# SyncE fetches one packed tile in six row by row, beside ScalarE's, in a graph layer on one Trainium2 core

## The chip, the cores and the metric

The kernel runs on one core of one Trainium2 chip. The metric is the time of one execution in microseconds (us) on the device, as a median of runs. The engines are called PE (TensorE), DVE (VectorE), ACT (ScalarE), POOL (GpSimd) and SP (SyncE). A queue name such as ACTq or SPq stands for what that engine's instruction stream issues to the DMA engines.

## What is computed

A graph layer over 12500 nodes of 128 features and 212500 edges, sorted by destination. Each edge carries the source node's row, multiplied by one of eight matrices that its type selects; the results are summed at the destination; a GRU cell updates the node; a residual and a layer norm follow. Cut to the core:

```python
all_msgs = jnp.einsum('nh,thd->ntd', h, message_W) + message_b
msg = all_msgs[src, edge_type]
messages = jax.ops.segment_sum(msg, dst, num_segments=num_nodes)
gi = messages @ gru_w_ih.T + gru_b_ih          # split in i_r, i_z, i_n
gh = h @ gru_w_hh.T + gru_b_hh                 # split in h_r, h_z, h_n
r = sigmoid(i_r + h_r); z = sigmoid(i_z + h_z); n = tanh(i_n + r * h_n)
out = layernorm(x + (1 - z) * n + z * h)       # h is x
```

## The kernel before

**Tiles and rounds.** Edges are taken in tiles of 128. The first 187 tiles (rounds 0 to 10, 17 tiles each) are "early". While they run, DVE packs the other edges on the chip (edges from a node to itself are taken out), and from round 11 on each round takes 16 packed tiles. There are 98 rounds, 0 to 97 (LAST), all written out without a loop. A round has three groups, of 6, 5 and 5 tiles in the packed part (GROUPS). Round r also finishes node tiles of some rounds before: the gates of node tile r-2, and the update and norm of r-3.

**A tile's way.** The 128 source rows of a tile, 512 bytes each, are brought from x in DRAM into SBUF, node on partition. PE multiplies them by a one-hot matrix of (destination, type) into the PSUM bank of the group (`sum_tiles`, L1651). ACT copies the bank out (L726), PE applies the eight matrices (`apply_weights`, L1678), DVE adds the window to the running sums in SBUF (L1166).

**Who brings the rows.** Nearly all tiles come by an indirect DMA that POOL issues, one for a tile (L660, called from `gather_packed`). Even and odd packed rounds have row sets of their own: `rows` for rounds 11, 13, ..., `rows_other` for 12, 14, .... So POOL, before it gathers group c of round r, waits only until PE has done group c of round r-2. One tile in every six rounds, the last of group 2 in rounds 17, 23, ..., 95 (FETCH_ROUNDS, 14 rounds), is not gathered by POOL. ACT fetches it during the six rounds up to and with its own: `fetch_rows` reads row numbers from SBUF into registers and issues one DMA a row (L896), 16 rows at one place of the round and 8 at another (8 only in the last of the six). These rows go to slot 16 of `rows`, which is otherwise free. PE waits for them on the semaphore `fetched`. The row numbers themselves are brought by SP, one line of 128 numbers a tile (`load_fetch_index`, L561).

**SP's round.** From round 12 on SP runs `round_(r)`: load x_next for node tile r (L544, waits until PE has turned the one before, L1687), store the finished node tile r-3 (L557, waits for DVE's out_tile, L1271), load x_tile for node tile r-2 (L548, under the same condition, read by DVE at L1251 in the next round). After a fetch round it adds one L561.

**Order on the other engines.** In a packed round PE runs: turn x (L1687), counts (L1616), group 0, the weights of the round before (L1678, L1680), group 1, group 2, then the gates of node tile r-2 (L1697, L1709, L1712, L1717). ACT runs the update of r-3, `fetch_rows(r, 0)`, copies of counts and sums, and `fetch_rows(r, 1)` after group 1.

Of the kernel before, what the change touches and what calls it, by code (L numbers as in the profile page):

```python
# [5 lines left out]
P = 128  # L6
F32 = mybir.dt.float32
BF16 = mybir.dt.bfloat16
I32 = mybir.dt.int32
# [7 lines left out]
def gnn_kernel(nc, x, src, dst, etype, w_msg, b_msg, w_ih, w_hh, b_ih, b_hh, out):  # L17
    ds = bass.ds
    NODES, HID = x.shape
# [8 lines left out]
    LAG = 2  # L28


    EARLY = 11
# [21 lines left out]
    LAST = ROUNDS - 1  # L53
# [5 lines left out]
    SPARE_SLOT = ROUND  # L59
# [6 lines left out]
    FETCH_EVERY = 6  # L66
    FETCH_AHEAD, FETCH_BEHIND = 16, 8
    FETCH_ROUNDS = tuple(range(EARLY + FETCH_EVERY, LAST, FETCH_EVERY))
    FETCH_SLOT = (ROUND - 1) % ROW_TILES
    FETCH_STEP = FETCH_EVERY * ROUND // ROW_TILES  # L70
    FETCH_TILE = GROUPS[2] - 1
# [35 lines left out]
    with ctx:  # L107
        def sb(name, shape, dt=F32):
            return ctx.enter_context(nc.sbuf_tensor(name, shape, dt))
# [4 lines left out]
        def sem(name):  # L114
            return ctx.enter_context(nc.semaphore(name))
# [69 lines left out]
        w_hh_rows = sb("w_hh_rows", [P, 3, HID])  # L185
# [6 lines left out]
        bias_part = [sb(f"bias_part{n}", [1, 512], BF16) for n in range(PARTS)]  # L192
# [5 lines left out]
        rows = sb("rows", [P, EARLY_ROUND, HID])  # L198
# [23 lines left out]
        fetch_src = w_ih_rows[:, 0, :].bitcast(I32)  # L222
        fetch_index = bias_part[0][0:1, :].bitcast(I32).rearrange("o (s e) -> o s e", e=P)

        def sets(name, cols, dt=F32):
            return [sb(f"{name}{s}", [P, cols], dt) for s in range(2)]

# [93 lines left out]
        fetch_src_ready = sem("fetch_src_ready")  # L321
        fetch_index_in = [sem(f"fetch_index_in{s}") for s in range(2)]
        fetched = [sem(f"fetched{s}") for s in range(2)]
        tiles_first_ready = sem("tiles_first_ready")
        tiles_first_in = sem("tiles_first_in")
        packed_code_ready = sem("packed_code_ready")
# [10 lines left out]
        tiles_done = [sem(f"tiles_done{c}") for c in range(3)]  # L337
# [78 lines left out]
        offset_lots = [(row, a, min(row.shape[1], SPARE_TILE + 1 - a))  # L416
                       for row, a in ((gate_bias, 0), (bias_rest, 512), (bi_row, 1024))]
        assert offset_lots[-1][1] + offset_lots[-1][2] == SPARE_TILE + 1

        def fetches(r):  # L420
            return isinstance(r, int) and r in FETCH_ROUNDS

# [66 lines left out]
        def _(sp):  # L489
# [65 lines left out]
            def store_out(j, n=P, s=0):  # L555
                sp.wait_ge(out_ready, j + 1)
                sp.dma_start(out[ds(j * P, n), :], out_tile[s][0:n, :]).then_inc(out_stored, 16)  # L557

            def load_fetch_index(m):
                row = (m + 1) * FETCH_STEP + 1  # L560
                sp.dma_start(fetch_index[0:1, m % 2, :], fetch_src[row:row + 1, :]).then_inc(fetch_index_in[m % 2], 16)  # L561

            def round_(r):
                load_x(r)
                store_out(r - LAG - 1)
                load_x_tile(r - LAG)

            flag = load_flag(sp)
            with sp.If(flag):
                last = NODE_TILES - 1  # L570
                load_x(0)
                load_x_tile(0)
                sp.dma_start(x_tile[1][0:NODE_LAST, :], x[last * P:NODES, :]).then_inc(last_x_tile_in, 16)
                load_bias()
                load_x(1)
                sp.wait_ge(packing, AT["next"])
                with nc.allow_non_contiguous_dma(reason="the kind of the edge that follows the early ones"):
                    sp.dma_start(kinds_T[P - 1:P, EARLY_TILES - 1, 1:2], moves_f[0:1, 0:1]).then_inc(carried, 16)
                load_x(2)
                for r in range(LAG + 1, EARLY - 1):  # L580
                    round_(r)
                sp.wait_ge(tiles_first_ready, 1)
                sp.wait_ge(fields_turned, CHUNKS)
                sp.dma_start(first_packed[0:1, 0:PACKED_TILES].rearrange("o (r k) -> o r k", k=ROW_TILES),
                             row_tiles_first[0:ROWS, :]).then_inc(tiles_first_in, 16)
                sp.wait_ge(fields_turned, FIELDS * CHUNKS)
                sp.dma_start(loops_words.rearrange("o (p c) -> o p c", c=WINDOW),
                             zeros_f[0:ACC_ROWS // 2 // WINDOW, 0:WINDOW]).then_inc(loops_zero, 16)
                for r in range(EARLY - 1, EARLY + 1):
                    round_(r)  # L590
                sp.wait_ge(fetch_src_ready, 1)
                sp.wait_ge(bias_in, PARTS * 16)
                for m in range(2):
                    load_fetch_index(m)
                for r in range(EARLY + 1, LAST):
                    round_(r)
                    m = (r - EARLY) // FETCH_EVERY + 1
                    if fetches(r - 1) and m < len(FETCH_ROUNDS):
                        sp.wait_ge(tiles_done[2], r)
                        load_fetch_index(m)  # L600
                load_x(last, NODE_LAST)
                store_out(last - LAG - 1)
                load_x_tile(last - LAG)
                sp.dma_start(last_x_tile, x[(last - 1) * P:last * P, :]).then_inc(last_x_tile_in, 16)
                store_out(last - LAG)
                store_out(last - 1)
                store_out(last, NODE_LAST, 1)
                sp.wait_ge(out_stored, 16 * NODE_TILES)
# [36 lines left out]
        def _(pool):  # L645
# [30 lines left out]
            def gather_packed(r):  # L676
                for c, n, start in groups(r):
                    pool.wait_ge(tiles_done[c], r if r == EARLY else r - 1)
                    for k in range(start, start + n - (c == 2 and fetches(r))):
                        a = column(r, k)  # L680
                        gather((rows_other if other(r) else rows)[:, k, :], src_T[:, a:a + 1],
                               gathered_last[k] if r == LAST else (gathered_other if other(r) else gathered)[c])
# [10 lines left out]
            with pool.If(flag):  # L693
# [5 lines left out]
                for r in range(EARLY, ROUNDS):  # L699
                    gather_packed(r)  # L700
                pool.wait_ge(tiles_done[2], FETCH_ROUNDS[-1] + 1)
                gather(rows[:, SPARE_SLOT, :], src_T[:, SPARE_COL:SPARE_COL + 1], gathered_last[SPARE_SLOT])
# [851 lines left out]
        def _(pe):  # L1554
# [71 lines left out]
            def landed(r, c):  # L1626
                if r < EARLY:
                    return max(1, r - 1) * EARLY_GROUPS[c]
                alike = range(EARLY + other(r), r + 1, 2)
                left_out = sum(fetches(q) for q in alike) if c == 2 else 0  # L1630
                return (0 if other(r) else (EARLY - 2) * EARLY_GROUPS[c]) + len(alike) * GROUPS[c] - left_out

            def sum_tiles(r, c, offs):
                _, n, start = groups(r)[c]
                if r > 0:
                    pe.wait_ge(sums_copied[c], r)
                pe.wait_ge(onehot_ready[c], r + 1)
                ahead = isinstance(r, int) and r in (1, 2)
                place = (rows, rows_second, rows_third)[r] if ahead else rows_other if other(r) else rows
                if ahead:  # L1640
                    pe.wait_ge(gathered_ahead[c], r * n * 16)
                elif r < LAST:
                    pe.wait_ge((gathered_other if other(r) else gathered)[c], landed(r, c) * 16)
                for k in range(n):
                    if r == LAST:
                        pe.wait_ge(gathered_last[start + k], 16)
                    slot = start + k
                    if fetches(r) and c == 2 and k == FETCH_TILE:
                        m, slot = (r - EARLY) // FETCH_EVERY - 1, SPARE_SLOT
                        pe.wait_ge(fetched[m % 2], (m // 2 + 1) * P * 16)  # L1650
                    last = nc.tensor.matmul(agg[c][:, ds(offs[c][k] * TYPES, CODES)],  # L1651
                                            place[:, slot, :],
                                            onehot[c][:, k, :], start=False, stop=True, skip_group_check=True)
                if isinstance(r, int) and r == LAST and c == 2:
                    pe.wait_ge(last_tile_ready, 3)
                    pe.wait_ge(gathered_last[SPARE_SLOT], 16)
                    last = nc.tensor.matmul(agg[2][:, ds(offs[3][0] * TYPES, CODES)], rows[:, SPARE_SLOT, :],
                                            onehot[1][:, GROUPS[1], :], start=False, stop=True, skip_group_check=True)
                last.then_inc(tiles_done[c], 1)
# [163 lines left out]
            with pe.Else():  # L1823
# [11 lines left out]
                with pe.Fori(0, EDGE_TILES) as i:  # L1835
# [5 lines left out]
                    for h, bank in enumerate((agg[2], cnt)):  # L1841
# [4 lines left out]
                                                start=False, stop=True)  # L1846
# [42 lines left out]
```

## Time and profile before

| | us |
|---|---|
| median of 3 runs | 1994.47 |
| lowest and highest | 1990.95, 1996.48 |
| profiled execution, own time | 1993.74 |
| its span | 1991.6 |

The times are of the whole execution. The profile's times count from the start of the span, which is 2.14 us shorter than the profiled execution's own time. Busy times are sums over an engine's instructions; "issue" is idle time for which the profile shows no releaser. A line of a timeline is: start, duration, engine, source line, operation, tiles written and read, how many were merged, and in brackets the idle time before it with what ended it.

### The profile page before, as it was taken

How to read it: one execution, taken by the hardware profiler on the slowest of the kernel's cores; microseconds unless marked ns; L12 is line 12 of the kernel's file. 1: busy time of each engine (PE TensorE's matmuls, PEld its weight loads, DVE VectorE, ACT ScalarE, POOL GpSimd, SP SyncE). 2: the span in 40 equal slices, each digit the busy share in tenths (PEclk: the TensorE clock that was granted, in tenths of full speed). 3: DMA queues.
4: the chain of work that ended last, by engine and by line, in shares of the span. 5: the costliest groups of instructions: out<-in, count | busy, mean ns of one | idle time of the engine just before them, and what ended most of it. 6: DMA issues, size and time to landing. Idle time of an engine off the chain costs nothing.

```text
span 1991.6 us, 34610 instructions
## 1 busy us (share of the span) xinstructions
PE 1372.3 (69%) x6657; PEld 1045.8 (53%) x6657; DVE 1245.0 (63%) x4650; ACT 595.0 (30%) x1489; POOL 1488.7 (75%) x1578
## 2 busy tenths in 40 slices
PE   1766676767676767676767777767676766766676
PEld 1755555555555555455545555545455555555554
DVE  7887465656565656565656566656565656565566
ACT  2323423232323232323232323232222323232222
POOL 7777777777777777777777777777777777777774
PEclk9877878888888888787878888888888888888889
DMA  5222222222222222222222222222222222222221
GB/s 128 58 62 64 56 64 65 66 62 64 63 66 61 65 63 65 62 65 62 66 61 66 63 65 63 64 63 65 63 64 63 64 63 63 63 65 63 64 63 45
DMA packets 100626, 128.44 MB, mean 64 GB/s; under 512 B 33280, under 2 KB 74959, under 8 KB 100478
## 3 DMA queue, kind: packets, MB, share of 16 engines
q0 software_dynamic: 50112, 102.73, 19.8%
q1 hardware_dynamic: 46584, 23.07, 4.2%
q10 hardware_dynamic: 3782, 0.93, 0.2%
q8 instruction: 61, 1.00, 0.2%
q14 instruction: 87, 0.71, 0.1%
HBM read 120.16 MB, written 6.40 MB: 64 GB/s over the span
## 4 chain that ended last, share of the span: by engine, by line
POOL 65%; issue 22%; DVE 8%; PE 3%; ACT 1%; DMA 1%; DVEq 0%; SPq 0%; ACTq 0%; POOLq 0%
POOL rows_other L660 33%; POOL rows L660 32%; DVE work L1317 1%; DVE codes L1314 1%; PE agg L1651 1%; DVE onehot L1150 1%; PE msg L1678 1%; DMA work<-in_src_dram 0%; DVE root_a L1224 0%; DVE messages_T L1166 0%; ACT sums_room L726 0%; ACT agg L726 0%; DVEq L1157 0%; PE gates L1717 0%; PE turn L1733 0%
## 5 line engine op out<-in xcount | busy, mean ns | idle before, releaser
L660 POOL DMA_INDIRECT rows<-in_x_dram,src_T x843 | 801.2, 950 | 260.9 <-issue 256.1
L660 POOL DMA_INDIRECT rows_other<-in_x_dram,src_T x688 | 651.8, 947 | 209.8 <-issue 209.8
L1651 PE MATMUL agg<-onehot,rows 128*128 128x128 f32 x1714 | 288.0, 330 | 256.9 <-DMA rows<-in_x_dram,src_T 255.9
L1678 PE MATMUL msg<-sums_room,w_type 128*128 128x320 f32 (+1 forms) x1552 | 443.1, 442 | 13.8 <-issue 10.3
L1651 PE MATMUL agg<-onehot,rows_other 128*128 128x128 f32 x1376 | 232.7, 330 | 259.6 <-DMA rows_other<-in_x_dram,src_T 258.3
L1651 PEld LDWEIGHTS agg<-onehot,rows 128*128 128x128 f32 x1714 | 259.6, 236 | 277.6 <-issue 276.6
L1678 PEld LDWEIGHTS msg<-sums_room,w_type 128*128 128x128 f32 x1552 | 306.2, 205 | 122.3 <-issue 27.0
L1199 DVE SCALAR_TENSOR_TENSOR sums_room<-turn,x_turned 128x128 f32<-128x128 f32 x696 | 145.6, 281 | 350.7 <-PE turn L1697 350.7
L1651 PEld LDWEIGHTS agg<-onehot,rows_other 128*128 128x128 f32 x1376 | 208.2, 235 | 278.5 <-issue 278.5
L726 ACT ACTIVATE sums_room<-agg 128x512 f32<-128x512 f32 x293 | 173.3, 591 | 375.7 <-PE agg L1651 327.6
L1150 DVE TENSOR_TENSOR onehot<-code_T,codes 128x640 f32<-128x640 f32 (+1 forms) x294 | 244.3, 859 | 18.9 <-PE agg L1651 18.8
L726 ACT ACTIVATE x_turned<-cnt 128x128 f32<-128x128 f32 x97 | 26.9, 277 | 670.9 <-PE msg L1680 573.9
L726 ACT ACTIVATE agg<-zeros_f 128x512 f32<-128x512 f32 x294 | 176.6, 601 | 9.4
L1138 DVE TENSOR_TENSOR node_mask<-rel_T,codes 128x320 bf16<-128x320 f32 (+3 forms) x294 | 139.1, 473 | 0.0
L1712 PE MATMUL gates<-w_hh_T,x_T 128*128 128x384 f32 x194 | 126.8, 751 | 0.0
L1166 DVE TENSOR_TENSOR messages_T<-messages_T,msg 128x64 f32 x291 | 63.9, 219 | 79.3 <-PE msg L1680 46.8
L1717 PE MATMUL gates<-w_ih_T,messages 128*128 128x384 f32 x194 | 107.5, 646 | 1.9 <-DVE messages L1207 1.9
L1177 DVE TENSOR_TENSOR loop_counts<-counts,loop_row 1x192 f32<-1x192 f32 x87 | 30.4, 350 | 97.1 <-ACT loop_row L726 87.6
L1616 PEld LDWEIGHTS cnt<-node_mask,type_mask 128*128 128x128 bf16 (+1 forms) x783 | 64.4, 105 | 47.6 <-issue 24.7
L1616 PE MATMUL cnt<-node_mask,type_mask 128*128 128x128 bf16 (+1 forms) x783 | 86.9, 228 | 0.0
L1717 PEld LDWEIGHTS gates<-w_ih_T,messages 128*128 128x128 f32 x194 | 54.5, 282 | 51.4 <-issue 42.8
L1181 DVE TENSOR_TENSOR work<-work,loop_counts 1x64 f32 x261 | 56.4, 216 | 37.3 <-DVE loop_counts L1177 0.2
(219 smaller groups left out, 1357.0 us busy)
## 6 DMA issues: line engine op xcount, KB each, us to landing
rows<-in_x_dram ACTq DMA_DIRECT2D x1792, 0.5 KB
rows<-in_x_dram,src_T POOLq DMA_INDIRECT x843, 2.5
rows_other<-in_x_dram,src_T POOLq DMA_INDIRECT x688
x_next<-in_x_dram SPq DMA_DIRECT2D x97, 64.0 KB
out_dram<-out_tile SPq DMA_DIRECT2D x97, 64.0 KB
x_tile<-in_x_dram SPq DMA_DIRECT2D x96, 64.0 KB
work<-in_dst_dram SPq DMA_DIRECT2D x1, 609.4 KB
work<-in_src_dram SPq DMA_DIRECT2D x1, 609.4 KB
```

The lines of the kernel that those rows point to most:

```text
L660: nc.gpsimd.indirect_dma_start(out=to, out_offset=None, in_=x[:, :], in_offset=bass.IndirectOffsetOnAxis(ap=index, axis=0),).then_inc(done ...
L726: return nc.scalar.activation(to, value, ACT.Copy)
L1138: nc.vector.tensor_tensor(node_mask[c][:, 0:n, 0:wide], rel_T[:, cols].unsqueeze(2).broadcast_to([P, n, wide]), codes[:, 0:wide].unsqueeze ...
L1150: nc.vector.tensor_tensor(onehot[c][:, 0:n, :], code_T[:, ds(column(r, start), n)].unsqueeze(2).broadcast_to([P, n, CODES]), codes[:, 0:CO ...
L1166: ins = nc.vector.tensor_tensor(messages_T[:, ds(node, WINDOW)], messages_T[:, ds(node, WINDOW)], bank[:, c * WINDOW:(c + 1) * WINDOW], AL ...
L1181: ins = nc.vector.tensor_tensor(loops_T[:, ds(node, WINDOW)], loops_T[:, ds(node, WINDOW)], (loop_counts if since(r, EARLY) else counts)[0 ...
L1199: done = nc.vector.scalar_tensor_tensor(out=to[:, t, :], in0=turn[:, 0:P], scalar=t - NO_LOOP, in1=values, op0=ALU.is_equal, op1=ALU.mult)
L1616: last = nc.tensor.matmul(cnt[0:m * HALF, c * P:c * P + m * WINDOW], type_mask[c][:, k:k + m, :].rearrange("p k t -> p (k t)"), node_mask[ ...
L1651: last = nc.tensor.matmul(agg[c][:, ds(offs[c][k] * TYPES, CODES)], place[:, slot, :], onehot[c][:, k, :], start=False, stop=True, skip_gr ...
L1678: nc.tensor.matmul(msg[:, 0:cols], w_type[:, t, :], sums[:, t, 0:cols], start=t == 0, stop=False, skip_group_check=True)
L1712: nc.tensor.matmul(bank[:, HID:4 * HID], x_lhs, w_hh_T[:, :], start=False, stop=False)
L1717: nc.tensor.matmul(gates_of(j)[:, 0:GATE], value, w_ih_T[:, :], start=False, stop=True).then_inc(gates_ready, 1)
```

## The change

SP takes over the last tile of group 2 in 13 further rounds: 20, 26, ..., 92 (SYNC_ROUNDS), which lie three rounds apart from ACT's. In these rounds POOL gathers 15 tiles rather than 16. SP fetches the 128 rows over six rounds, 8 right after its x_next load and 16 after its x_tile load (8 in all in the last of the six), each with a DMA of its own whose row number is read from SBUF into a register. The rows go to a room of their own, 512 bytes a partition that held a part of w_hh, which nobody reads after the start. PE waits for them on `sync_fetched` ahead of that tile's product. The 128 row numbers of each tile come by one more small load on SP; from the second tile on it stands behind a wait of SP for `tiles_done[2]` at r. All that ACT fetches stays as it was.

```diff
+    SYNC_ROUNDS = tuple(range(EARLY + FETCH_EVERY + FETCH_EVERY // 2, LAST, FETCH_EVERY))
...
+        sync_index = bias_part[1][0:1, :].bitcast(I32).rearrange("o (s e) -> o s e", e=P)
+        sync_room = w_hh_rows[:, 0, :]
...
+            def load_sync_index(m):
+                row = (m + 1) * FETCH_STEP + FETCH_STEP // 2 + 1
+                sp.dma_start(sync_index[0:1, m % 2, :], fetch_src[row:row + 1, :]).then_inc(sync_index_in[m % 2], 16)
+
+            def sync_rows(r, behind):
+
+                m, step = divmod(r - EARLY - FETCH_EVERY // 2 - 1, FETCH_EVERY)
+                if m < 0 or m >= len(SYNC_ROUNDS) or behind and sync_fetches(r):
+                    return
+                a = step * (FETCH_AHEAD + FETCH_BEHIND) + behind * FETCH_BEHIND
+                n = FETCH_AHEAD if behind else FETCH_BEHIND
+                if step == 0 and not behind:
+                    sp.wait_ge(sync_index_in[m % 2], (m // 2 + 1) * 16)
+                    if m > 0:
+                        sp.wait_ge(tiles_done[2], r)
+                        if m + 1 < len(SYNC_ROUNDS):
+                            load_sync_index(m + 1)
+                _, numbers = nc.values_load_multi_w_load_instructions(
+                    sync_index[0:1, m % 2, a:a + n], engines=[sp.engine], min_val=0, max_val=NODES - 1,
+                    skip_runtime_bounds_check_because="row numbers, as the gathers take them")
+                for p, number in enumerate(numbers, a):
+                    sp.dma_start(sync_room[p:p + 1, :], x[ds(number, 1), :]).then_inc(sync_fetched[m % 2], 16)
...
                 for m in range(2):
                     load_fetch_index(m)
+                    load_sync_index(m)
                 for r in range(EARLY + 1, LAST):
-                    round_(r)
+                    load_x(r)
+                    sync_rows(r, 0)
+                    store_out(r - LAG - 1)
+                    load_x_tile(r - LAG)
+                    sync_rows(r, 1)
...
-                    for k in range(start, start + n - (c == 2 and fetches(r))):
+                    for k in range(start, start + n - (c == 2 and (fetches(r) or sync_fetches(r)))):
...
-                left_out = sum(fetches(q) for q in alike) if c == 2 else 0
+                left_out = sum(fetches(q) or sync_fetches(q) for q in alike) if c == 2 else 0
...
+                    elif sync_fetches(r) and c == 2 and k == FETCH_TILE:
+                        m, tile_rows = (r - EARLY) // FETCH_EVERY - 1, sync_room
+                        pe.wait_ge(sync_fetched[m % 2], (m // 2 + 1) * P * 16)
```

## Rows read from the trace of the kernel before

**Rows 1.** The page's first part: span, and busy time of each engine.

```profile
span 1991.6 us, 34610 instructions
PE 1372.3 (69%) x6657; PEld 1045.8 (53%) x6657; DVE 1245.0 (63%) x4650; ACT 595.0 (30%) x1489; POOL 1488.7 (75%) x1578
```

**Rows 2.** The page's chain that ended last, shares of the span by engine.

```profile
POOL 65%; issue 22%; DVE 8%; PE 3%; ACT 1%; DMA 1%; DVEq 0%; SPq 0%; ACTq 0%; POOLq 0%
```

**Rows 3.** Groups of instructions on POOL, 262 us to 1972 us: count, busy, mean ns, idle.

```profile
L660 POOL DMA_INDIRECT rows_other<-in_x_dram,src_T x688 | 651.8, 947 | 209.8 <-issue 209.8
L660 POOL DMA_INDIRECT rows<-in_x_dram,src_T x678 | 642.1, 947 | 206.8 <-issue 206.8
```

**Rows 4.** POOL's timeline: last wait for PE, an ACT-fetch round, a plain round, the end.

```profile
243.64 0.94 POOL L660 DMA_INDIRECT rows<-in_x_dram,src_T  x1 [3.54 <-PE agg L1651]
...
602.79 0.94 POOL L660 DMA_INDIRECT rows<-in_x_dram,src_T  x1 [0.30 <-issue]
...
620.28 1.11 POOL L660 DMA_INDIRECT rows<-in_x_dram,src_T  x1 [0.31 <-issue]
621.69 0.94 POOL L660 DMA_INDIRECT rows_other<-in_x_dram,src_T  x1 [0.30 <-issue]
...
641.69 0.94 POOL L660 DMA_INDIRECT rows<-in_x_dram,src_T  x1 [0.30 <-issue]
...
1949.18 0.94 POOL L660 DMA_INDIRECT rows_other<-in_x_dram,src_T  x1 [0.30 <-issue]
...
1970.41 0.94 POOL L660 DMA_INDIRECT rows<-in_x_dram,src_T  x1 [0.30 <-issue]
```

**Rows 5.** PE's timeline over that ACT-fetch round and the start of the next.

```profile
608.95 0.27 PE L1687 MATMUL cnt<-ident,x_next 128*128 128x128 f32 x1
609.05 0.95 PE L1616 MATMUL cnt<-node_mask,type_mask 128*128 128x128 bf16 x9
611.65 1.58 PE L1651 MATMUL agg<-onehot,rows 128*128 128x128 f32 x12 [1.65 <-DMA rows<-in_x_dram,src_T]
613.07 4.47 PE L1678 MATMUL msg<-sums_room,w_type 128*128 128x320 f32 x16
617.38 0.49 PE L1680 MATMUL msg<-counts,b_type 128*128 128x192 f32 x2
618.03 1.35 PE L1651 MATMUL agg<-onehot,rows 128*128 128x128 f32 x10 [0.16 <-DMA rows<-in_x_dram,src_T]
623.02 2.48 PE L1651 MATMUL agg<-onehot,rows 128*128 128x128 f32 x10 [3.64 <-DMA rows<-in_x_dram,src_T]
...
628.57 0.27 PE L1687 MATMUL cnt<-ident,x_next 128*128 128x128 f32 x1
```

**Rows 6.** Groups on PE, 262 us to 1950 us: the tile products and their waits.

```profile
L1651 PE MATMUL agg<-onehot,rows_other 128*128 128x128 f32 x1366 | 231.2, 330 | 256.1 <-DMA rows_other<-in_x_dram,src_T 254.7 <-issue 0.2
L1651 PE MATMUL agg<-onehot,rows 128*128 128x128 f32 x1376 | 230.0, 328 | 238.7 <-DMA rows<-in_x_dram,src_T 237.8
```

**Rows 7.** ACT's timeline around its row fetches.

```profile
610.71 0.28 ACT L842 ACTIVATE gates<-t_pre 128x128 f32<-128x128 f32 x1 [0.93 <-DVE t_pre L1240]
611.60 3.03 ACTq L896 DMA_DIRECT2D rows<-in_x_dram  x8
...
629.89 0.28 ACT L842 ACTIVATE gates<-t_pre 128x128 f32<-128x128 f32 x1 [0.48 <-DVE t_pre L1240]
631.24 6.08 ACTq L896 DMA_DIRECT2D rows<-in_x_dram  x16
```

**Rows 8.** SP's timeline, two rounds with the next start, then its tightest later round.

```profile
609.25 0.33 SPq L544 DMA_DIRECT2D x_next<-in_x_dram  x1
615.41 0.34 SPq L557 DMA_DIRECT2D out_dram<-out_tile  x1
615.80 0.43 SPq L548 DMA_DIRECT2D x_tile<-in_x_dram  x1
628.87 0.33 SPq L544 DMA_DIRECT2D x_next<-in_x_dram  x1
634.59 0.34 SPq L557 DMA_DIRECT2D out_dram<-out_tile  x1
634.98 0.43 SPq L548 DMA_DIRECT2D x_tile<-in_x_dram  x1
635.46 0.51 SPq L561 DMA_DIRECT2D bias_part<-w_ih_rows  x1
...
728.49 0.33 SPq L544 DMA_DIRECT2D x_next<-in_x_dram  x1
734.43 0.34 SPq L557 DMA_DIRECT2D out_dram<-out_tile  x1
734.82 0.45 SPq L548 DMA_DIRECT2D x_tile<-in_x_dram  x1
745.19 0.33 SPq L544 DMA_DIRECT2D x_next<-in_x_dram  x1
```

**Rows 9.** SP's own waits, 262 us to 1950 us: total, times, longest.

```profile
SPq L544 <- PE cnt L1687: 1109.5, 86, 19.9
SPq L557 <- DVE out_tile L1271: 463.6, 83, 7.0
```

**Rows 10.** DVE's timeline: the reader of x_tile.

```profile
630.30 0.29 DVE L1251 TENSOR_TENSOR t_d<-x_tile,gates 128x128 f32<-128x128 f32 x1 [0.44 <-ACT gates L842]
```

**Rows 11.** Busy time in stretches; the last three columns are PEclk, DMA share, GB/s.

```profile
265.00:1950.00 1685.00, 1184.33 (x5620) 888.06 (x5620) 1025.29 (x3928) 494.66 (x1278) 1274.83 (x1346) 0.84 0.24 64
```

**Rows 12.** Groups on POOL, 1950 us to 1972 us, where ACT fetches no rows.

```profile
L660 POOL DMA_INDIRECT rows<-in_x_dram,src_T x17 | 16.1, 945 | 5.2 <-issue 5.2
```

**Rows 13.** The page's DMA queues: packets, MB, share of 16 engines' span.

```profile
q10 hardware_dynamic: 3782, 0.93, 0.2%
```

**Rows 14.** PE's timeline at the end: last wait for a gather, and the last rounds' products.

```profile
1951.79 1.46 PE L1651 MATMUL agg<-onehot,rows_other 128*128 128x128 f32 x10 [3.56 <-DMA rows_other<-in_x_dram,src_T]
...
1974.57 1.28 PE L1651 MATMUL agg<-onehot,rows 128*128 128x128 f32 x10
```

More of the change, by code:

```diff
@@ L323, in gnn_kernel @@
         fetched = [sem(f"fetched{s}") for s in range(2)]
+        sync_index_in = [sem(f"sync_index_in{s}") for s in range(2)]
+        sync_fetched = [sem(f"sync_fetched{s}") for s in range(2)]
         tiles_first_ready = sem("tiles_first_ready")
@@ L418, in gnn_kernel, with sync_fetches @@
         assert offset_lots[-1][1] + offset_lots[-1][2] == SPARE_TILE + 1
+        def sync_fetches(r):
+            return isinstance(r, int) and r in SYNC_ROUNDS
         def fetches(r):
@@ L1646, in sum_tiles @@
                         pe.wait_ge(gathered_last[start + k], 16)
-                    slot = start + k
+                    tile_rows = place[:, start + k, :]
                     if fetches(r) and c == 2 and k == FETCH_TILE:
-                        m, slot = (r - EARLY) // FETCH_EVERY - 1, SPARE_SLOT
+                        m, tile_rows = (r - EARLY) // FETCH_EVERY - 1, rows[:, SPARE_SLOT, :]
                         pe.wait_ge(fetched[m % 2], (m // 2 + 1) * P * 16)
+                    elif sync_fetches(r) and c == 2 and k == FETCH_TILE:
+                        m, tile_rows = (r - EARLY) // FETCH_EVERY - 1, sync_room
+                        pe.wait_ge(sync_fetched[m % 2], (m // 2 + 1) * P * 16)
                     last = nc.tensor.matmul(agg[c][:, ds(offs[c][k] * TYPES, CODES)],
-                                            place[:, slot, :],
+                                            tile_rows,
                                             onehot[c][:, k, :], start=False, stop=True, skip_group_check=True)
```

## The prediction, made before the changed kernel ran

> **What bounds the kernel now.** I read the busy times first [rows 1]: POOL is the busiest engine, but 75% alone would leave a quarter of the span open. The chain that ended last closes that gap [rows 2]: 65% of the span is POOL and 22% is "issue", 87% together. The groups on POOL say what this issue time is [rows 3]: 1366 gathers of 947 ns, and before them 209.8 + 206.8 = 416.6 us of idle time, all of it "issue", so 305 ns ahead of each gather and no wait for any engine. The timeline gives the same [rows 4]: POOL waits for PE the last time at 243.64 us and then issues one gather after another. One gather costs POOL 947 + 305 = 1252 ns. A plain round of 16 gathers, from 621.69 to 641.69 us [rows 4], gives 20.00 / 16 = 1.250 us. Whatever takes one gather out of this stretch, and leaves nothing else late, takes 1.25 us out of the time.
>
> PE follows behind. Its products of tiles wait 254.7 + 237.8 = 492.5 us for landings in 262 to 1950 us [rows 6], over 85 rounds 5.8 us each. In a round these waits lie at 1.65, 0.16 and 3.64 us ahead of the three groups [rows 5]. The small one is no sign of a bound: PE may be late for group 1 as long as it has caught up at group 2, where 3.64 us are left. And POOL doesn't feel PE's lag. It starts to refill `rows` at 641.69, where PE had read group 0 of that set from 611.65 for 1.58 us: 28.5 us of room.
>
> **What is removed.** 13 gathers, in rounds 20, 26, ..., 92. All of them lie behind 243.64 us and ahead of 1949.18, so on the chain. 13 x 1.252 = **16.3 us**. That a round with 15 gathers is really shorter is shown by ACT's fetch round: POOL starts `rows` at 602.79 and the next set at 621.69, so 18.90 us, with one long gather of 1.11 us among the 15; the plain round behind it lasts 641.69 - 621.69 = 20.00 us [rows 4]. The difference is 1.10 us, and 1.26 us without the 0.16 us of the long gather. The rest of that round on PE bears it too: group 2 with the fetched tile takes 2.48 us with nothing between its ten products [rows 5], so a wait for fetched rows ahead of the fifth tile costs nothing where the rows are there.
>
> **The end.** It moves as a whole. The last wait for a gather is at 1951.79, for the gather of 1949.18; from there on PE is never again held by POOL [rows 14], though the last gather is issued until 1971.35 (1970.41 + 0.94). By the 1.67 us that passed between the end of the gather of 1949.18 (1950.12) and its landing at 1951.79, that last one lands at about 1973.0, and PE takes up the products that need it at 1974.57. Its margin of 1.5 us stays, since POOL and PE both arrive 16.3 us earlier; nothing of the gain is lost there. The end's 1991.6 - 1951.8 = 39.8 us stay as they are.
>
> **What is added on SP.** 24 rows a round in five rounds of six and 8 in the sixth, over 78 rounds (15 to 92). SP issues no such DMA before, so the price is ACT's: 6.08 us for 16 and 3.03 us for 8, 0.38 us a row, and between the last work and the first row 631.24 - 630.17 = 1.07 us for 16 register loads and 611.60 - 610.99 = 0.61 us for 8 [rows 7]. Bounds for a row on SP: its own shortest DMA is 0.33 us and its own longest 0.51 us [rows 8]. I take 0.38, since it is the same kind of instruction; the range keeps both ends. SP's round is then:
> x_next 0.33, registers 0.61, 8 rows 3.03: SP is ready for the store 3.97 us after the start. It now starts the store 615.41 - 609.25 = 6.16 us after, held by DVE's out_tile; over all rounds this wait is 463.6 / 83 = 5.6 us [rows 9]. So the 3.64 us disappear in it, with 2 us to spare. At 0.51 us a row it would be 4.7 of 5.6 us: still hidden.
> Store 0.34, x_tile 0.43 to 0.45, registers 1.07, 16 rows 6.08: the last two, 7.15 us, come ahead of the next x_next. The room there is 628.87 - 616.23 = 12.6 us in the shown round, 1109.5 / 86 = 12.9 us on average [rows 9], and 745.19 - 735.27 = 9.9 us in the tightest round behind 300 us [rows 8]. At 0.51 us it would be 9.2 us, just inside.
> A whole SP round is 0.33 + 0.61 + 3.03 + 0.34 + 0.43 + 1.07 + 6.08 = 11.9 us of the 19.6 us between two x_next loads. What is queued behind the rows keeps its time: the store and x_tile wait for DVE anyway, x_tile issued at 615.80 is read at 630.30 [rows 10], and x_next of 609.25 at 628.57 [rows 5].
> **SP's new wait** for `tiles_done[2]` at r is met when it is reached: SP has just passed the wait for PE's turn in round r (L1687), and PE does that turn after group 2 of round r-1. Behind it are the index load (0.51 us, 13 in all, two of them at the start of round 12 beside ACT's two) and the 8 rows; 3.97 + 0.51 = 4.5 us is still under 5.6. Cost nothing.
>
> **What is added on PE and the DMA engines.** Thirteen waits on PE, in rounds with 3.6 us or more of room. The last 8 rows of a tile are issued from 0.9 us to 4.0 us after PE's turn; PE reaches the fifth tile of group 2 some 15 us after it (623.02 + 4/5 x 2.48 - 608.95 = 16.1 us). ACT's last 8 go out 0.6 us later than that (611.60 to 614.63) and are in time. The traffic is small: ACT's 1792 rows are q10's 3782 packets, at 0.2% of 16 engines' span [rows 13], so 0.002 x 16 x 1991.6 = 64 us or 36 ns a row. 1664 rows more are 59 us of DMA time, spread over 1500 us. The 16 DMA engines are busy 24% of the time [rows 11].
> **A gather beside them** could take longer. The nearest rows: 947 ns while ACT fetches [rows 3] and 945 ns where it doesn't [rows 12]. Were SP's rows to add the same 2 ns to all 1366 gathers, that is 2.7 us; below, a gain isn't to be had, for the 945 ns are as low as any. I take nothing, since single gathers spread more (0.94 to 1.11), and keep 2.7 us in the range.
>
> Sum: 1993.74 - 16.3 = 1977.4 us for an execution like the profiled one. The median of the runs shown is 0.73 us above the profiled execution: 1994.47 - 16.3 = **1978.2 us**, 0.8% faster.
>
> **A rule that speaks against it.** What would be bound if the DMA engines were full, not POOL? The trace says 24% busy and 1.25 us a gather on POOL [rows 3, 11]. The Trainium skill, page "DMA: Bandwidth & Descriptors", section "Issuing engines are not separate DMA queues", says that DMAs started on several engines run on the same 16 DMA engines, and that spreading them saves only the starting engine's time, "which is usually small relative to the DMA itself". By that rule the change would bring nothing and the time would stay 1994.5 us. Here the rule's first half may well hold, but not its "small": the starting time is what fills POOL.
>
> **Rivals.**
> 1. *SP becomes the bound, slower than before.* A row costs SP much more than ACT. SP's round is 2.8 us plus 24 rows, against a round of 19.6 us, so it decides from (19.6 - 2.8) / 24 = 0.70 us a row. At 0.80 us SP's round is 22.0 us against the 20.0 of a plain one, in 65 rounds of 24 rows: 65 x 2.0 = 130 us more, 2124 us. Against it: SP's own DMAs of 128 rows each take 0.33 to 0.51 us. Chance 0.03.
> 2. *Gathers stretch and eat the gain: no change.* The gain is gone if 1366 gathers take 16.3 / 1366 = 12 ns more each, by more descriptors on the shared engines: 1994.5 us. For it: POOL's work is itself a DMA's start, and the rule above; against it: the 2 ns between stretches with and without ACT's rows. A half-way form, 6 ns, would give 1986 us. Chance 0.05 for a loss beyond 10 us.
> 3. *PE waits for SP's rows.* Rows that go out in single DMAs behind 64 KB transfers on the same queue could land 12 us late. Then PE stands in 13 rounds; but since POOL has 28 us of room, only PE's own lag counts, which 3.6 us a round take back. Only a wait of over 28 us reaches POOL. Time 1978 us as in the forecast, so it changes nothing but a wait. Its bad form, rows missing for more than that: chance 0.01, slower.
>
> **Chances.** Forecast, faster: 0.91. Rival 2, within 0.3%: 0.05. Rivals 1 and 3, slower: 0.03 + 0.01 = 0.04. A difference of 0.3%, 6 us, is about what a measurement of this kernel can tell from no change. The forecast's own range is 1978.2 less 3 us and plus 2.7 + 3 us, where 3 us is the spread of the runs before around their median (1990.95 to 1996.48): 1975 to 1984. I widen it a little below, for a disturbance that the median of three holds: 1974 to 1984.
>
> **What would show it.** Right: 13 gathers fewer on POOL, each still 945 to 948 ns with 305 ns idle; "issue" the only releaser; rounds of 18.8 us at every third place and of 20.0 between them; SP with 1664 row DMAs at 0.33 to 0.51 us; SP's wait at L544's place fallen from 12.9 to about 5.8 us on average, at L557's from 5.6 to about 2; the wait on PE a little smaller (about 5.6 us a round) and always for gathers. Wrong: x_next late on PE, an idle time on POOL that PE ends, a gather mean above 950 ns, or a PE wait that ends with `sync_room`.

## The result, and the profile after the change

The changed kernel took 1975.4 us (median of 4 runs, 1974.54 to 1976.46), the kernel before 1994.0 us. The ratio is 0.991 (95% interval 0.9897 to 0.9922): 0.9% faster, where 1978.2 us and 0.8% had been forecast. Two later comparisons, told below, gave 0.9909 (0.9892 to 0.9926) and again 0.9909 (0.9893 to 0.9926).

The span and the chain of the changed kernel, to be laid beside [rows 1, 2]:

```profile
span 1973.7 us, 39661 instructions
PE 1356.7 (69%) x6561; PEld 1050.8 (53%) x6657; DVE 1248.0 (63%) x4650; ACT 594.6 (30%) x1489; POOL 1474.7 (75%) x1565
...
POOL 65%; issue 22%; DVE 8%; PE 3%; ACT 1%; DMA 1%; DVEq 0%; SPq 0%; ACTq 0%; POOLq 0%
```

POOL has 13 instructions less (1565 for 1578), and the chain is made of the same parts: what bounded the kernel bounds it still. POOL's groups from 262 us to 1956 us answer to [rows 3]:

```profile
L697 POOL DMA_INDIRECT rows<-in_x_dram,src_T x676 | 639.5, 946 | 206.2 <-issue 206.2
L697 POOL DMA_INDIRECT rows_other<-in_x_dram,src_T x675 | 638.1, 945 | 205.9 <-issue 205.9
```

There is still no releaser but "issue", so POOL never waited in this stretch. POOL's timeline, the first gather of round 12 and the last of round 96, answers to the end in [rows 4]:

```profile
263.22 0.94 POOL L697 DMA_INDIRECT rows_other<-in_x_dram,src_T  x1 [0.30 <-issue]
...
1929.11 0.94 POOL L697 DMA_INDIRECT rows_other<-in_x_dram,src_T  x1 [0.30 <-issue]
```

In the kernel before the same two stood at 265.04 and 1949.18 us:

```profile
265.04 0.95 POOL L660 DMA_INDIRECT rows_other<-in_x_dram,src_T  x1 [0.30 <-issue]
```

That a round with 15 gathers is the shorter one shows in the first gathers of rounds 31, 32 and 33, of which 32 is one of SP's:

```profile
637.09 0.94 POOL L697 DMA_INDIRECT rows<-in_x_dram,src_T  x1 [0.30 <-issue]
...
657.08 0.94 POOL L697 DMA_INDIRECT rows_other<-in_x_dram,src_T  x1 [0.30 <-issue]
...
675.96 0.94 POOL L697 DMA_INDIRECT rows<-in_x_dram,src_T  x1 [0.30 <-issue]
```

Round 31 takes 19.99 us and round 32 takes 18.88.

So the 17.9 us between the spans (1991.6 - 1973.7) come apart in three: the stretch between these gathers fell from 1684.14 to 1665.89 us, by 18.25; what lies ahead of it is 1.82 us shorter (265.04 to 263.22); what lies behind, from the last of them to the end of the span, is 2.17 us longer (42.42 to 44.59).

SP's own part, two rounds of its timeline in the changed kernel, beside [rows 7, 8]:

```profile
604.80 0.36 SPq L553 DMA_DIRECT2D x_next<-in_x_dram  x1
606.10 3.48 SPq L589 DMA_DIRECT2D w_hh_rows<-in_x_dram  x8
610.85 0.38 SPq L566 DMA_DIRECT2D out_dram<-out_tile  x1
611.28 0.42 SPq L557 DMA_DIRECT2D x_tile<-in_x_dram  x1
613.09 6.48 SPq L589 DMA_DIRECT2D w_hh_rows<-in_x_dram  x16
624.47 0.36 SPq L553 DMA_DIRECT2D x_next<-in_x_dram  x1
```

16 rows take 6.48 us, 0.405 a row here; the 8 take 3.48 us, 0.435 a row, but most batches of 8 take about 3.15. The register loads lie in the gaps: 606.10 - 605.16 = 0.94 us for 8, and 613.09 - 611.70 = 1.39 us for 16. After the last row, at 619.57, SP stands idle for 4.9 us until the next x_next. The waits of SP from 262 us to 1935 us answer to [rows 9]:

```profile
SPq L553 <- PE cnt L1727: 567.0, 86, 20.4
SPq L566 <- DVE out_tile L1308: 140.4, 84, 6.8
```

Ahead of x_next 567.0 / 86 = 6.6 us are left of 12.9, ahead of the store 140.4 / 84 = 1.7 us of 5.6. The new work went into SP's waits, as it was meant to.

### The profile page after: what moved, and what is told of

It reads as the page before. It is cut to its first block, busy times and chain, and to the rows that moved or that the text cites. A ratio compares the mean times of both kernels' runs of the same rounds, so it can differ in the third digit from the quotient of the medians.

```text
span 1973.7 us, 39661 instructions
## 1 busy us (share of the span) xinstructions
PE 1356.7 (69%) x6561; PEld 1050.8 (53%) x6657; DVE 1248.0 (63%) x4650; ACT 594.6 (30%) x1489; POOL 1474.7 (75%) x1565
## 4 chain that ended last, share of the span: by engine, by line
POOL 65%; issue 22%; DVE 8%; PE 3%; ACT 1%; DMA 1%; DVEq 0%; SPq 0%; ACTq 0%; POOLq 0%
POOL rows L697 32%; POOL rows_other L697 32%; DVE work L1354 1%; DVE codes L1351 1%; PE agg L1691 1%; DVE onehot L1187 1%; PE msg L1718 1%; DMA work<-in_src_dram 0%; PE msg L1836 0%; DVE root_a L1261 0%; DVE messages_T L1203 0%; ACT sums_room L763 0%; PE turn L1773 0%; ACT agg L763 0%; DVEq L1194 0%
## 5 line engine op out<-in xcount | busy, mean ns | idle before, releaser
L697 POOL DMA_INDIRECT rows_other<-in_x_dram,src_T x675 | 638.1, 945 | 205.9 <-issue 205.9
L1691 PE MATMUL agg<-onehot,rows_other 128*128 128x128 f32 x1350 | 224.6, 326 | 230.5 <-DMA rows_other<-in_x_dram,src_T 229.0
L1691 PEld LDWEIGHTS agg<-onehot,rows_other 128*128 128x128 f32 x1350 | 200.9, 231 | 248.2 <-issue 248.1
L1187 DVE TENSOR_TENSOR onehot<-code_T,codes 128x640 f32<-128x640 f32 (+1 forms) x294 | 245.2, 863 | 18.2 <-PE agg L1691 18.2
L1757 PE MATMUL gates<-w_ih_T,messages 128*128 128x384 f32 x194 | 115.1, 688 | 2.2 <-DVE messages L1244 2.2
```

What stands on the lines that cost most here:

```text
L697: nc.gpsimd.indirect_dma_start(out=to, out_offset=None, in_=x[:, :], in_offset=bass.IndirectOffsetOnAxis(ap=index, axis=0),).then_inc(done ...
L1187: nc.vector.tensor_tensor(onehot[c][:, 0:n, :], code_T[:, ds(column(r, start), n)].unsqueeze(2).broadcast_to([P, n, CODES]), codes[:, 0:CO ...
L1757: nc.tensor.matmul(gates_of(j)[:, 0:GATE], value, w_ih_T[:, :], start=False, stop=True).then_inc(gates_ready, 1)
```

## The experiments

Two theories were to be told apart. Mine: the time is POOL's count of gathers times 1.25 us, and SP's rows cost nothing. The rival: SP's rows do something to the gathers or to the loads, and the sum only happens to come out. Beside them stood the question from which point SP's own time binds. The lines of these kernels are numbered a little differently; the names are the same.

**First chip.** The first four kernels ran together on a chip on which the kernel before took 2451.2 us. It has no trace there; in the kernels that have one, POOL isn't what bounds them. They are told first, since they showed something that no later run did.

*The cost alone.* POOL gathers all tiles as before and PE reads POOL's copy, while SP fetches its rows and PE waits for them:

```diff
-                    for k in range(start, start + n - (c == 2 and (fetches(r) or sync_fetches(r)))):
+                    for k in range(start, start + n - (c == 2 and fetches(r))):
...
-                        m, tile_rows = (r - EARLY) // FETCH_EVERY - 1, sync_room
+                        m = (r - EARLY) // FETCH_EVERY - 1
                         pe.wait_ge(sync_fetched[m % 2], (m // 2 + 1) * P * 16)
```

> The cost alone: SP fetches its 1664 rows and PE waits for them, but POOL gathers all tiles as before and PE reads POOL's copy. My theory (only POOL's gathers set the time, SP's rows are hidden): as before, 1994 us, within 2 us; gathers of 945 to 948 ns. Rival (SP's rows change how long a gather takes): with the 1.5 ns less a gather that the changed kernel's trace shows, 1992 us; with 12 ns more, 2010 us.

It took 2609.3 us, ratio 1.0632 (1.0602 to 1.0662) to the kernel before on that chip. Neither theory had this.

*The gain alone.* POOL leaves out the 13 gathers, and `load_sync_index` and `sync_rows` are not called:

```diff
-                        m, tile_rows = (r - EARLY) // FETCH_EVERY - 1, sync_room
-                        pe.wait_ge(sync_fetched[m % 2], (m // 2 + 1) * P * 16)
+                        tile_rows = sync_room
```

> The gain alone: POOL leaves out the 13 gathers and SP fetches nothing; PE multiplies what lies in the room, without a wait, so the rows of these 13 tiles are left out of the result. My theory: 1994 - 13 x 1.25 = 1977.7 us, and at most 2 us from the changed kernel's 1975.4, so 1975 to 1978. Rival (SP's rows cost something that is hidden in the sum, by shared DMA engines or late loads): clearly below the changed kernel, 1970 us or less.

It took 2430.4 us, ratio 0.9919 (0.9897 to 0.994). The ratio is much like the forecast's, but POOL isn't the bound there, and in what way 13 gathers less shorten this kernel is not shown. The chain of this kernel on that chip, by engine and by line, shows ACT's row fetches (L930) in POOL's place:

```profile
issue 33%; ACTq 33%; ACT 12%; DVE 9%; PE 8%; another core or an unknown queue 2%; DVEq 1%; DMA 0%; SPq 0%
ACTq L930 28%; ACT sums_room L760 5%; ACTq L926 4%; PE msg L1714 3%; PE agg L1687 2%; ACT counts L760 2%; ACT loop_row L760 1%; ACT gates L876 1%; PE gates L1753 1%; DVEq L1191 1%; PE gates L1748 1%; ACT agg L760 1%; DVE onehot L1184 1%; DVE work L1351 1%
```

A row is three instructions on ACT: two of registers, then the DMA. The durations of the first and the last of them (ns, lowest, median and highest), first in the changed kernel where the kernel before takes 1994 us, then in this one on the first chip:

```profile
L933 ACTq FUSED_REGOPS  x1792: 37/37/37, 279.7 to 1903.3; - x200
L933 ACTq DMA_DIRECT2D rows<-in_x_dram x1792: 213/213/668, 279.8 to 1903.4; - x200
```

```profile
L930 ACTq FUSED_REGOPS  x1792: 3/37/1151, 381.5 to 2368.3; - x200
L930 ACTq DMA_DIRECT2D rows<-in_x_dram x1792: 3/213/1396, 381.6 to 2368.3; - x200
```

The median is the same, but some take over a microsecond, and the register instruction among them, which moves nothing. So a full DMA queue can't be all of it. The chain in order of time shows such a stretch, one piece after another at 0.7 us, ahead of ACT's next copy:

```profile
1021.83 0.71 ACTq L930
1022.55 0.69 ACTq L930
1023.26 0.69 ACTq L930
1023.96 0.71 ACTq L930
1024.69 0.69 ACTq L930
```

A gather costs its usual price there (944 to 947 ns in this kernel too, with 0.3 us of issue ahead of most). What is slow is the pace of the streams in which many short instructions follow each other. With SP's rows beside it (the cost alone) both streams have it: 16 rows of SP take a median of 16.2 us, against 6.49 us for the same kernel on the third chip. The chain turns to SP:

```profile
SPq 43%; issue 40%; PE 6%; DVE 5%; another core or an unknown queue 2%; ACTq 2%; ACT 1%; DMA 1%; DVEq 0%
```

*Each SP row twice,* the second copy into a room that nobody reads; PE waits for both:

```diff
-                    sp.dma_start(sync_room[p:p + 1, :], x[ds(number, 1), :]).then_inc(sync_fetched[m % 2], 16)
+                    for room in (sync_room, w_hh_rows[:, 1, :]):
+                        sp.dma_start(room[p:p + 1, :], x[ds(number, 1), :]).then_inc(sync_fetched[m % 2], 16)
...
-                        pe.wait_ge(sync_fetched[m % 2], (m // 2 + 1) * P * 16)
+                        pe.wait_ge(sync_fetched[m % 2], (m // 2 + 1) * 2 * P * 16)
```

> The changed kernel with each SP row fetched twice, the second copy to a room that nobody reads: 48 row DMAs a round in five of six. In the changed kernel a row costs SP 0.405 us, 16 register loads 1.39 us and 8 of them 0.94 us. SP's round becomes 0.36 + 0.38 + 0.42 + 0.94 + 1.39 + 48 x 0.405 = 22.9 us against 18.8 to 20.0. Theory of SP's limit: five rounds of 22.9 and one of about 16, in which POOL's ahead rows are used up, so 130.5 us in place of 117.5, thirteen times: 2145 us (2100 to 2180), POOL waits for PE, PE for x_next. Rival (SP's issue time is never the bound, rows only share the DMA engines): 1975 to 1985 us.

*One tile in four rounds,* with two rooms in turn; the tile of the round is chosen so that its row numbers lie in the copied column:

```diff
-    SYNC_ROUNDS = tuple(range(EARLY + FETCH_EVERY + FETCH_EVERY // 2, LAST, FETCH_EVERY))
+    SYNC_EVERY = 4
+    SYNC_ROUNDS = tuple(range(EARLY + 7, LAST, SYNC_EVERY))
+    SYNC_TILE = (15, 11, 7)
...
-                m, step = divmod(r - EARLY - FETCH_EVERY // 2 - 1, FETCH_EVERY)
+                m, step = divmod(r - SYNC_ROUNDS[0] + SYNC_EVERY, SYNC_EVERY)
...
+                a, n = step * 32 + behind * 16, 16
```

> SP fetches one tile in four rounds rather than one in six, 32 rows in each round (16 behind x_next, 16 behind x_tile), into two rooms in turn: 20 gathers of POOL are left out rather than 13. SP's round: 0.36 + 0.38 + 0.42 + 2 x 1.39 + 32 x 0.405 = 16.9 us, under the shortest round of 18.75. My theory: 1975.4 - 7 x 1.25 = 1966.6 us (1964 to 1969). Rival (SP's store comes too late, as 16 rows and their registers are 7.9 us against the 6.2 us after which the store is due, and DVE and PE wait): 1975 us or more.

On the first chip they took 3104.3 us (1.2668) and 2916.8 us (1.1903). The more row DMAs SP issues, the slower: 1664 of them gave 2609 us, 2560 gave 2917 and 3328 gave 3104. The changed kernel itself didn't run on that chip; that it is slower there is likely by the 1.0632 of its rows alone, but wasn't measured.

**Second chip.** The changed kernel again, and a kernel in which POOL leaves out one tile in every round from 12 to 96, so 58 more, and PE multiplies w_hh in its place (no SP row is added):

```diff
+        def left_out_tile(r):
+            return fetches(r) or sync_fetches(r) or EARLY < r < LAST
...
-                    for k in range(start, start + n - (c == 2 and (fetches(r) or sync_fetches(r)))):
+                    for k in range(start, start + n - (c == 2 and left_out_tile(r))):
```

> The changed kernel unchanged, beside the kernel before on the same chip. On the chip of the first four experiments the kernel before took 2451 us, not 1994, and 49% of its variant's chain was the row DMAs' own instructions on ACT, of which many take 0.70 us rather than 0.21. If this chip does the same, POOL isn't the bound and the changed kernel should take about what the rows alone took there, 2600 us, 6% more than before; if the kernel before takes 1994 us here, the changed one takes 1975.

The 49% of this expectation is the share of a stretch of 30 us; over the whole span it is 28%, as shown above.

> The changed kernel, in which POOL also leaves out the last tile of group 2 in the 58 other rounds from 12 to 96; PE multiplies what lies in a part of w_hh instead, so these rows are left out of the result. Where the kernel before takes 1994 us: POOL is still the bound at 18.75 us a round, 1975.4 - 58 x 1.25 = 1903 us (1899 to 1908). Rival (another engine is the bound just below 19.6 us a round): 1940 us or more. Where the row DMAs' streams are the bound: no change against the changed kernel, 2600 us.

The changed kernel took 1975.9 us against 1994.5, the other 1902.8 us (1900.2 to 1904.3), on the forecast of 1903. So the price of a gather, (1975.9 - 1902.8) / 58 = 1.26 us, holds down to a round of 18.8 us, and no second bound lies in between. Of the waits of this kernel, 262 us to 1860 us, two say how much is left on PE:

```profile
PE agg L1696 <- DMA rows_other<-in_x_dram,src_T: 206.2, 100, 3.8
PE agg L1696 <- DMA rows<-in_x_dram,src_T: 200.2, 87, 3.7
```

406.4 us over some 85 rounds, 4.8 us in each, for 5.8 in [rows 6]. With 71 gathers less in 85 rounds a round is 1.05 us shorter on average, and nearly all of that was taken out of these waits.

**Third chip.** The first four kernels again, on a chip where the kernel before took 1993.8 us.

> The same kernel as e1_rows_only (SP fetches its rows, POOL gathers all tiles as well), for a chip on which the kernel before takes 1994 us. Theory of POOL's gathers alone: 1994 us within 2 us, with gathers of 945 to 948 ns. Rival (SP's rows change the length of a gather): 1992 us at 1.5 ns less, 2010 us at 12 ns more. On a chip like that of the first four, 6% more than before again.

1993.75 us, ratio 0.9997 (0.9987 to 1.0007). SP's rows cost nothing here, to a tenth of a per cent, with gathers of 946 and 947 ns:

```profile
L697 POOL DMA_INDIRECT rows_other<-in_x_dram,src_T x688 | 650.8, 946 | 209.9 <-issue 209.9
L697 POOL DMA_INDIRECT rows<-in_x_dram,src_T x678 | 642.0, 947 | 206.8 <-issue 206.8
```

> The same kernel as e2_gathers_out: POOL leaves out the 13 gathers, SP fetches nothing, and the rows of these 13 tiles are left out of the result. Where the kernel before takes 1994 us: 1975 to 1978 us by my theory, 1970 us or less if SP's rows cost something hidden in the changed kernel's 1975.

1974.4 us, ratio 0.9903 (0.9886 to 0.9919), where the changed kernel has 0.991 (0.9897 to 0.9922). It is 0.6 us below the forecast of 1975 to 1978 and above the rival's 1970. The whole gain is that of the 13 gathers, and both halves give the whole within their intervals: 0.9997 x 0.9903 = 0.990.

> The same kernel as e4_every_four: SP fetches one tile in four rounds, 32 rows a round, 20 gathers are left out. Where the kernel before takes 1994 us: SP's round is 16.9 us, under the shortest round of 18.75, so 1975.4 - 7 x 1.25 = 1966.6 us (1964 to 1969). Rival (the late store or SP's issue time holds the round): 1975 us or more.

1967.4 us, ratio 0.9868 (0.9851 to 0.9884); the forecast was 1966.6.

> The same kernel as e3_rows_twice: 48 row DMAs of SP a round in five rounds of six. Where the kernel before takes 1994 us: SP's round is 22.9 us against 18.8 to 20.0, in the sixth round PE catches up to its own pace, so 2145 us (2100 to 2180), with POOL waiting for PE and PE for x_next. Rival (SP's issue time is never the bound): 1975 to 1985 us.

2011.5 us (2008.8 to 2014.1), ratio 1.0091 (1.0069 to 1.0112). SP is over its limit and the kernel is slower than before, but by 36 us against the changed kernel and not by 170. Its chain rests on SP:

```profile
SPq 58%; issue 20%; DVE 8%; PE 6%; POOL 3%; ACT 2%; DMA 1%; ACTq 1%; DVEq 1%; POOLq 0%
```

SP's timeline in this kernel:

```profile
1004.51 0.37 SPq L553 DMA_DIRECT2D x_next<-in_x_dram  x1
1005.81 5.72 SPq L590 DMA_DIRECT2D w_hh_rows<-in_x_dram  x16
1011.58 0.37 SPq L566 DMA_DIRECT2D out_dram<-out_tile  x1
1012.01 0.42 SPq L557 DMA_DIRECT2D x_tile<-in_x_dram  x1
1013.81 11.95 SPq L590 DMA_DIRECT2D w_hh_rows<-in_x_dram  x32
1025.81 0.55 SPq L594 DMA_DIRECT2D bias_part<-w_ih_rows  x1
1026.41 0.58 SPq L553 DMA_DIRECT2D x_next<-in_x_dram  x1
```

Two things in my expectation were wrong. The second copy shares its register instruction, so a DMA costs 5.72 / 16 = 0.36 us and not 0.405; and SP doesn't have to keep each round, only the six together. A full round is 0.37 + 0.93 + 5.72 + 0.37 + 0.42 + 1.38 + 11.95 = 21.1 us, the sixth 0.37 + 0.93 + 5.72 + 0.37 + 0.42 = 7.8, in sum 113.5 us against the 117.5 of six rounds. SP falls behind in five rounds and comes back in the sixth. What that costs is seen in the waits, 262 us to 1950 us:

```profile
PE agg L1692 <- DMA w_hh_rows<-in_x_dram: 194.4, 13, 18.8
DVE t_d L1289 <- DMA x_tile<-in_x_dram: 131.0, 35, 5.8
...
POOL rows_other L698 <- PE agg L1692: 23.0, 7, 4.7
POOL rows L698 <- PE agg L1692: 2.1, 4, 0.8
```

PE waits for the last rows of the tile 13 times, 194.4 / 13 = 15 us each. POOL's two row sets keep most of that away from POOL, which waits 25.1 us. The rest of the loss is at the end. Of the 38.7 us between this span and the changed kernel's, 20.9 lie in the stretch from round 12 to the last gather of round 96, and 15.9 behind it (60.45 us for 44.59). The window behind that gather shows why: PE has 210 products left where it has 131 in the changed kernel, some 80 more.

```profile
1951.95:2012.40 60.45, 41.35 (x210) 31.41 (x211) 42.17 (x174) 17.31 (x48) 16.98 (x18) 0.85 0.13 34
```

PE's wait for the rows of round 92 ended at 1906.85 us and was the longest, 18.8 us, and PE didn't catch up again. This is the prediction's third rival, brought about by SP's lag. It doesn't run as the prediction had it: there only a wait of over 28 us was to cost time, and here none reached 19.

**Fourth chip: the changed kernel and the one of four rounds side by side.**

> The changed kernel on the same chip as e7_four_pair. Where the kernel before takes 1994 us: 1975 to 1976 us. Where it takes 2451 us, as on the chip of the first four runs: 2590 to 2620 us, as the rows alone did there, since POOL isn't the bound there and 13 gathers less bring nothing.

> The kernel of e4b_every_four beside the changed kernel on one chip. Where the kernel before takes 1994 us: 7 gathers of 1.25 us less than the changed kernel, 1967 us (1964 to 1969), so 0.4% below it. Where the kernel before takes 2451 us: 2900 us as before.

The kernel before took 1993.6 us, the changed one 1975.4 us (0.9909, 0.9893 to 0.9926), the one of four rounds 1967.0 us (0.986, 0.9843 to 0.9876): 8.4 us less by 7 gathers, 1.2 us each. It beats the changed kernel where the streams run at their usual pace. SP's waits in it (third chip, 262 us to 1940 us) show how near the limit it is:

```profile
SPq L565 <- PE cnt L1742: 222.1, 74, 18.1
SPq L578 <- DVE out_tile L1322: 27.0, 6, 5.9
```

222.1 us over some 85 rounds are 2.6 us of room in each, and the store is nearly always late now (it waited for DVE only 6 times), which costs nothing.

## Why the prediction was right

**The bound and its price.** The chain, the 305 ns of issue time ahead of each gather, and 1.252 us a gather held: 58 more gathers gave 1.26 us each, 7 gave 1.2, and 13 with nothing else changed gave the change's whole gain.

**The sum.** It was 16.3 us; the measured medians differ by 18.6, the spans by 17.9. In this profile the step that was a little short is "a gather beside them". It was taken at no change and bounded by nothing below. The 1351 gathers behind 262 us took 945.7 ns in place of 947.2. Per gather, 1684.14 us over 1345 intervals is 1.2522 us before and 1665.89 over 1332 is 1.2507 after: 1.5 ns x 1332 = 2.0 us, which with the 16.3 make the 18.25 of the stretch. The profiles don't show that as an effect of the change: the other two of the changed kernel give 1.2530 and 1.2509 us, the 13 gathers left out alone 1.2528, SP's rows with all gathers 1.2515. The groups of the changed kernel on the second chip, with a span of 1977.1 us:

```profile
L697 POOL DMA_INDIRECT rows<-in_x_dram,src_T x678 | 642.9, 948 | 206.9 <-issue 206.9
L697 POOL DMA_INDIRECT rows_other<-in_x_dram,src_T x675 | 639.5, 947 | 206.0 <-issue 206.0
```

But chance isn't shown either. All four comparisons with 13 gathers less gave more than 16.3 us: 18.6, 18.6 and 18.2, and 19.4 without SP's rows. With 71 gathers less it was 91.7 us for 88.9. Each interval reaches down to the forecast, yet all lie on the same side. 0.3 us of it lies outside the span (own time less span is 2.14 us before and 1.83 after); where the rest comes from stays open. So the forecast was right in its mechanism and its size, and about 2 to 3 us short in each of these comparisons.

**The end.** I said it moves as a whole. It is 2.17 us longer in this profile. The windows from the last wait for a gather to the end, the kernel before and then the changed one (the third number from the right is the granted clock as a share of 2.4 GHz):

```profile
1951.80:1991.60 39.80, 26.66 (x133) 19.65 (x133) 25.60 (x111) 7.92 (x24) 14.99 (x16) 0.90 0.15 40
```

```profile
1931.70:1973.70 42.00, 29.01 (x131) 22.07 (x133) 25.64 (x111) 7.92 (x24) 15.12 (x16) 0.83 0.15 38
```

DVE and ACT did the same work in the same time; PE's busy time rose from 26.66 to 29.01 us at a mean granted clock of 0.83 rather than 0.90 of 2.4 GHz. Up to here POOL hides such a difference, and in the end nothing does. The other two profiles of the changed kernel have 43.2 and 43.3 us from the last gather of round 96 to the end, at a clock of 0.84, where this one has 44.59 and the one before 42.42. What lies ahead of round 12 is 1.82 us shorter here, but varies as well: that round's first gather starts at 264.89 and 261.66 us in those two profiles. So the two parts nearly cancel by luck.

**SP.** A row costs 0.405 us and not 0.38, and the registers 0.94 and 1.39 us rather than 0.61 and 1.07. The row lies within the bounds that were kept for it; for the registers no upper bound had been given. All stayed hidden. Two readings of the prediction were off without a consequence: the 0.51 us among "SP's own DMAs of 128 rows each" is the load of one line of row numbers, and by its own terms ACT's last 8 rows go out 1.4 us later than SP's (611.60 against 610.19), not 0.6. The wait ahead of the store came out as forecast (1.7 for "about 2"), the one ahead of x_next at 6.6 us for 5.8. There the forecast had taken the 7.15 us off every round, though the sixth has no rows behind and 8 of the 86 have none at all: 12.9 - 7.15 x 65 / 86 = 7.5, less what the rows cost more.

**PE.** Its waits for landings came to 231.1 + 229.0 = 460.1 us from 262 us to 1935 us, 5.4 us in each of 85 rounds for the 5.6 forecast, and PE has no wait for `sync_room` (in the trace `w_hh_rows`) at all. The waits of the changed kernel:

```profile
PE agg L1691 <- DMA rows<-in_x_dram,src_T: 231.1, 96, 5.4
PE agg L1691 <- DMA rows_other<-in_x_dram,src_T: 229.0, 96, 5.0
```

**The page's rule.** "DMA: Bandwidth & Descriptors" of the Trainium skill would have the change bring nothing, since another issuing engine saves only issue time, "usually small relative to the DMA itself". The trace disagrees with the second half: the gain is the time that POOL spends on issuing 13 gathers, 16.3 us, to within 2.3 us.

**The rivals.** *Gathers stretch* fell by the cost alone (0.9997). *SP becomes the bound* is a real mechanism, at 48 rows a round and not at 24, but its price was worked out wrongly: it charged each round's excess to the time, 130 us at 0.80 us a row, where the sixth, light round gives nearly all of it back. By the same sum over six rounds a row could have cost (117.5 - 5 x 2.8 - 1.7) / (5 x 24 + 8) = 0.80 us before SP's work exceeds the time at all. That is an upper end: with each row twice the work was 113.5 us of 117.5, and 36 us were lost already. *PE waits for SP's rows* comes first on that way, and was given too little weight as SP's companion. And no rival had the first chip, where the row fetches bind and their instructions come slowly.

## What to carry to other kernels

Where one engine issues back to back with only "issue" between, its count times its step is the time: each piece of work handed to an engine that stands in a wait is worth one step. That ends before the other engine's work over a whole period fills the period, for what it brings last comes late. Handing over by many short instructions has a price that the profile of one chip need not show, so a gain of 1% of this kind should be measured on several. And the last stretch, where the leading engine is done, varies by itself (42.4 to 45.0 us behind the last gather of round 96, in the nine profiles in which nothing holds POOL), and nothing hides it.

## What the runs showed of the hardware

On the first chip all five kernels were 22% to 56% above the 1994 us that the kernel before takes on the others, where it took 2451 us. A gather took 944 to 947 ns and ACT's copy of a group 590 ns, as elsewhere; the products with the eight matrices took 512 ns on average for 442, at a mean granted clock of 0.78 for 0.84 of 2.4 GHz, with PE busy for a smaller share of the time. The row instructions on ACT took up to 1.4 us there, register instructions up to 1.15 us among them (1.38 us with SP's rows beside them), against 37 ns at all times in the traces of the other chips. ACT's batches of 8 rows took a median of 8.1 us in the kernel without SP's rows, for 3.0 us in the kernel before and the changed one elsewhere. In the same trace POOL waits 177.5 us for releases that the profile calls "remote", of which the traces of the other chips show none. What slows the streams is open: the pieces of 0.7 us one after another look like instructions that arrive one by one, but no view shows their arrival, and no later run fell on that chip. The Trainium skill says on its page "Runtime: NRT & Kernel Launch", section "Instruction fetch mechanics", that fetching is hidden because an engine dispatches more slowly than it is filled. If fetching is the cause, this chip speaks against it; no run here can tell.
